# Sharing the place comparisons of an attention value pass between VectorE and GpSimd

## The reference, cut to what matters

```
score = einsum('ehd,ehd->eh', K[src], Q[dst]) / sqrt(32) + edge_bias
m = segment_max(score, dst)
ex = exp(score - m[dst])
denom = segment_sum(ex, dst)
attn = ex / denom[dst]
out = segment_sum(attn[:, :, None] * V[src], dst)
```

## Time and profile before

| | |
|---|---|
| Median of three timed runs | 7159.44 us |
| The profiled execution | 7132.51 us |
| Its span | 7130.8 us |
| GpSimd busy | 4465.6 us (63%) |
| TensorE busy | 4317.0 us (61%) |
| VectorE busy | 3165.0 us (44%) |
| Mean granted TensorE clock | 0.781 |

### The profile page before, as it was taken

How to read it: one execution, slowest core, us unless ns; L and a number is a source line. 1 busy time by engine, 2 the same in 40 slices (tenths; PEclk the granted TensorE clock), 3 DMA queues, 4 the chain that set the end, 5 groups by cost and what they waited for, 6 DMA issues and landing times. The chain is left out here.

```text
span 7130.8 us, 75257 instructions
## 1 busy us (share of the span) xinstructions
PE 4317.0 (61%) x20054; PEld 2955.9 (41%) x20055; DVE 3165.0 (44%) x6539; ACT 1916.6 (27%) x4343; POOL 4465.6 (63%) x4304
## 2 busy tenths in 40 slices
PE   1000588888766666668896455455477767775555
PEld 1000365656534444445674333233344434443333
DVE  5040345544446888878644222222244433333443
ACT  2630355555424555446461000000000000000000
POOL 2677566666546888746313666666566646665666
PEclk6555788888778899989997676767688878887766
DMA  3112122222105666657103445454455544443333
GB/s 85 46 41 54 55 65 67 66 66 67 42 25 178 210 210 213 189 168 215 43 0 122 145 147 140 147 147 146 129 170 176 176 114 133 131 134 97 97 97 87
DMA packets 466880, 826.73 MB, mean 116 GB/s; under 512 B 146229, under 2 KB 316182, under 8 KB 460057
## 3 DMA queue, kind: packets, MB, share of 16 engines
q0 software_dynamic: 209808, 566.12, 27.9%
q1 hardware_dynamic: 256777, 256.98, 11.3%
HBM read 664.90 MB, written 157.90 MB: 115 GB/s over the span
## 5 line engine op out<-in xcount | busy, mean ns | idle before, releaser
L1349 POOL DMA_INDIRECT p_rows<-table,idx_s x1320 | 1292.0, 979 | 773.7 <-issue 372.2
L1394 PE MATMUL p_psA<-p_rows,p_hot 128*128 128x256 bf16 (+1 forms) x4840 | 895.0, 349 | 602.1 <-DMA p_rows<-table,idx_s 401.7
L1394 PEld LDWEIGHTS p_psA<-p_rows,p_hot 128*128 128x128 bf16 (+1 forms) x4840 | 622.1, 134 | 856.2 <-issue 714.3
L585 POOL DMA_INDIRECT p_space<-h_table,p_space x440 | 451.6, 1026 | 289.5 <-issue 126.9
L571 POOL DMA_INDIRECT rec_s<-p_rec_out,p_row_s x416 | 429.8, 1033 | 283.0 <-ACT p_rec_out L696 138.3
L1349 POOL DMA_INDIRECT p_rows<-rel_table,edge_d x440 | 433.8, 986 | 254.0 <-issue 126.2
L655 PE MATMUL p_psW<-p_wf,p_upto 128*128 128x256 f32 x1760 | 480.1, 434 | 183.9 <-DVE p_upto L815 163.3
L376 POOL DMA_INDIRECT rec_d<-edge_d,norm x416 | 426.4, 1025 | 238.2 <-issue 125.3
L1557 POOL DMA_INDIRECT p_rows<-rel_table,edge_d x440 | 437.8, 995 | 219.3 <-issue 129.9
L1423 ACT ACTIVATE sums<-p_psA,inv_degree 128x256 f32<-128x256 f32 x75 | 35.6, 474 | 1850.7 <-DMA p_locs<-loc_rows 963.0
L1777 POOL DMA_INDIRECT p_kg<-kv_table,edge_d x440 | 425.1, 966 | 165.2 <-issue 111.6
(11 more groups left out here) (354 smaller groups left out, 8749.8 us busy)
## 6 DMA issues: line engine op xcount, KB each, us to landing
v_sorted<-p_kg SPq DMA_DIRECT2D x110, 512.0 KB
p_val<-v_sorted SPq DMA_DIRECT2D x110, 512.0 KB
rel_table<-p_o SPq DMA_DIRECT2D x50, 1024.0 KB
p_rows<-table,idx_s POOLq DMA_INDIRECT x1320
p_space<-rec_s SPq DMA_DIRECT2D x110, 136.0 KB
p_locs<-loc_rows SPq DMA_DIRECT2D x110, 128.0 KB, 4.3
p_rows<-rel_table,edge_d POOLq DMA_INDIRECT x880
p_rec_out<-edge_attr SPq DMA_DIRECT2D x103, 128.0 KB
```

The source lines that it names most:

```text
L585: pool.indirect_dma_start(msg[q][:, u, :], None, table, bass.IndirectOffsetOnAxis(ap=rec_i[q][:, u, S_IDX:S_IDX + 1], axis=0))\
L1349: pool.indirect_dma_start(rows[q][:, u, :], None, table, bass.IndirectOffsetOnAxis(ap=idx(n * U + u), axis=0))\
L1394: step = pe.matmul(psA[:, bass.ds(at[u], D)], hot[q][:, u, :], rows[q][:, u, c * D:(c + 1) * D], start=False, stop=(c == terms - 1), skip_ ...
```

## The change

VectorE compares the places of the even groups only, still six groups ahead. GpSimd compares those of the odd groups, with the same operation on the same operands, five groups ahead of its own products. The semaphore `shown` becomes two, one per engine, and both TensorE and SyncE wait for the one that belongs to their group.

```diff
+        shown = [s.sem(n) for n in ("shown_by_dve", "shown_by_pool")]
+
+        def wait_shown(engine, n):
+
+            engine.wait_ge(shown[n % 2], n // 2 + 1)
+
+        def show(engine, n):
+
+            engine.wait_ge(shown_in[n % LR], n // LR * 16 + 16)
+            if n >= TR:
+                engine.wait_ge(spread, n - TR + 1)
+            engine.tensor_scalar(hotT[n % TR][:, :, :], rows[n % LR][:, :, :], g.lane[:, 0:1], None, ALU.is_equal)\
+                .then_inc(shown[n % 2], 1)
...
                     if n >= LR:
-                        sp.wait_ge(shown, n - LR + 1)
+                        wait_shown(sp, n - LR)
...
-                unrolled(groups, [(0, weigh)])
+                def show_odd(n):
+                    if n % 2:
+                        show(pool, n)
+
+                unrolled(groups, [(5, show_odd), (0, weigh)])
...
-                    pe.wait_ge(shown, n + 1)
+                    wait_shown(pe, n)
...
-                def show(n):
-                    dve.wait_ge(shown_in[n % LR], n // LR * 16 + 16)
-                    if n >= TR:
-                        dve.wait_ge(spread, n - TR + 1)
-                    dve.tensor_scalar(hotT[n % TR][:, :, :], rows[n % LR][:, :, :], g.lane[:, 0:1], None, ALU.is_equal)\
-                        .then_inc(shown, 1)
+                def show_even(n):
+                    if n % 2 == 0:
+                        show(dve, n)
...
-                unrolled(groups, [(6, show), (5, join), (0, add(0)), (5, lower), (0, add(1)), (0, add(2)), (0, add(3)), (0, pick)])
+                unrolled(groups, [(6, show_even), (5, join), (0, add(0)), (5, lower), (0, add(1)), (0, add(2)), (0, add(3)), (0, pick)])
```

More of the change, by code:

```diff
@@ L1969, in value_pass @@
         shown_in = [s.sem(f"shown_in{q}") for q in range(LR)]
-        measured, hotted, shown, spread, joined, lowered, picked, expd, weighed, summed, added, blanked = (
-            s.sem(n) for n in ("measured", "hotted", "shown", "spread", "joined", "lowered", "picked", "expd", "weighed",
+        measured, hotted, spread, joined, lowered, picked, expd, weighed, summed, added, blanked = (
+            s.sem(n) for n in ("measured", "hotted", "spread", "joined", "lowered", "picked", "expd", "weighed",
                                "summed", "added", "blanked"))
+        shown = [s.sem(n) for n in ("shown_by_dve", "shown_by_pool")]
[7 more added lines that the diff above has]
+                .then_inc(shown[n % 2], 1)
         cleared, dve_step, ahead_in = s.sem("cleared"), s.sem("dve_step"), s.sem("ahead_in")
```

## The result

The changed kernel takes 7163.64 us in the median of 20 runs, the kernel before 7139.42 us in 20 runs beside it. The ratio is 1.0033 with a 95% interval of 1.0024 to 1.0042: about 24 us slower. The time lies inside the full range that was given, 7112 to 7182 us, but on the wrong side of before; the forecast was 11 us faster. The interval is 0.2% wide, so the sign can be told, although the change is smaller than the 0.5% that I had put as what a measurement can tell.

What follows compares the result with a forecast made beforehand. VectorE's chain bounds the stage at 5.92 us per period; the new loop of 4.9 + 0.8 = 5.7 us saves 0.22 us times 50, 11 us: 7159.4 - 11 = 7148 us, own range 7132 to 7162, full range 7112 to 7182.

Steps and rivals of the forecast that it cites:

- The bound before: Value stage: VectorE's own chain of eight additions, two comparisons, a join and a lower sets the period of 5.92 us.
- the 0.46 us per period that leave VectorE: Odd comparisons leaving VectorE cut its period from 5.92 to 5.46 us; times 50 periods, 23 us at most.
- The price of GpSimd's comparison, s: Time of one odd-group comparison on GpSimd, taken as 0.8 us between 0.62 and 1.57.
- The break-even at s = 1.02: GpSimd comparison time from which the changed kernel would be slower than before, in the forecast's order.
- The loop: VectorE's even comparison, expand, GpSimd's comparison, two products, next even comparison: 4.9 + s, 5.7 us per period.
- case B: GpSimd's comparison is slow, s = 1.57: loop 6.47 us, 27 us slower, 7187 us; chance 0.2.
- The stage's start: GpSimd's first comparisons fall in its idle time before the first exponents; no cost, or s once without this cover.
- case C: GpSimd's comparison starts before VectorE's lower, which stands still for s: period 6.23 us, 15 us slower, 7175 us; chance 0.2.
- the full gain: Rival A: loop 5.52 us or less, VectorE's 5.46 us the bound; 20 to 23 us faster, 7137 us; chance 0.17.
- Late places: Transfers for odd groups landing late: 5 us if one in ten is late; rival D, 7159 us, chance 0.08.
- The offset of 27 us between profile and median: Median of three timed runs lay 27 us above the profiled execution; the same offset was taken for the forecast.

Runs made afterwards that it cites:

- pair experiment: Kernel before, all comparisons on VectorE, but the odd one (seven groups ahead) directly behind the even one; ratio 0.9991 (0.9980 to 1.0002), period 5.73 us.
- the kernel with the comparisons in the gaps: Kernel before, all comparisons on VectorE, each moved into a wait between two additions; ratio 1.0081 (1.0064 to 1.0098), period about 7.0 us.

## Why the prediction was wrong

- **The bound before, and the 0.46 us per period that leave VectorE: right.** The pair experiment, where GpSimd is busy for only 65% of the time, gave 5.73 us (5.46 + 0.27). The 5.47 us of the kernel with more buffers agree with my 5.46, but prove less, since GpSimd's own work comes to 5.47 us there.
- **The price of GpSimd's comparison, s: this term failed.** I took 0.8 us between the bounds 0.62 and 1.57; it is 1.563. The upper bound came from the row of the same operation in the same type, 225 ns for one element and 370 for 56, and was exact within 0.01 us. I argued it away with its short rows and leaned on the memset and the affine select, which are other operations. The break-even at s = 1.02 lay between.
- **The loop: right in kind, 0.15 us too long.** I gave 4.9 + s; four kernels show 4.75 + s. The GpSimd comparison started 1.00 us after the products' end, not 1.07, and two products take 3.75 us from the comparison's end, not 3.83. With s = 1.563 my own sum gives 6.46 us and 27 us slower, case B, which had a chance of 0.2. Measured were 6.31 and 24. That 27 is so close to 24 is partly luck: the periods give only 20, and some 3 us come from the start of the stage.
- **The stage's start: a term that I had put at nothing.** I took GpSimd's first comparisons to fall into idle time. Two periods at the start cost 3.4 us more than before instead.
- **The lower's race, case C: the price was wrong.** I took it that VectorE's lower or comparison stands still beside any GpSimd instruction until that is over. It does beside a product. GpSimd's comparison holds it up only in its first half microsecond, by 0.43 us at most in the kernel with five hotT buffers, and not by s. So C's price of s on top doesn't exist, and the full gain was also to be had with s = 1.56 once the loop was open, which I hadn't seen.
- **Late places: near nothing.** In the changed kernel the places cost GpSimd 5.8 us of waiting, 4.0 of them in the stage's second period and 1.8 in one later period, of 7.12 us. They decide only with five hotT buffers.
- **The offset of 27 us between profile and median: wrong as an offset.** The kernel before had three runs then; with 20 its median is 7139, 7 us above the profiled one. It was the spread of the runs. It also lifted the predicted time: 11 us less than 7139 would have been 7128, and not 7148.

## What to carry to other kernels

Work given to an idle engine is paid by where it stands in the loops between engines, not by the idle time that it fills: ask for each new wait which instruction of the same period releases it, and whether that one can itself wait for the new work. Here more buffers, two of hotT and four of the places, turned 0.3% slower into 0.4% faster without another instruction. For a price that the trace doesn't show, take the row of the same operation and type, even a tiny one, before rows of the right size of another operation; and before giving work away, look whether the owner only does it at a bad moment.

## What the runs showed of the hardware

GpSimd's TENSOR_SCALAR takes 2.5 ns per element, by instructions of 256 and 512 elements in bf16 and of 256 in fp32, with a constant or a per-partition operand, so it is slower per element than GpSimd's two-input product (1.55 ns). The Trainium skill (GPSIMD Engine Reference, Performance versus the Vector engine) gives 769 ns for 512 elements at the best loop rate; the trace has 1563, and the measurement decides.

VectorE's comparison is held up by GpSimd's only near its start. In the kernel with more buffers of both kinds, one that starts 0.11 us into GpSimd's takes 0.72 us and one that starts 0.34 us into it 0.49 us; both end 0.83 us after the start of GpSimd's. One that starts 0.51 us or later into it takes the short duration, 0.34 to 0.35 us, in this kernel and in the one with five hotT buffers. Here is one that starts 0.34 us into GpSimd's comparison, and one that starts 0.90 us into it:

```profile
3269.77 1.56 POOL L1984 TENSOR_SCALAR p_hotT<-p_locs,lane 128x512 bf16<-128x512 bf16 x1
3270.11 0.49 DVE L1984 TENSOR_SCALAR p_hotT<-p_locs,lane 128x512 bf16<-128x512 bf16 x1
```

```profile
3263.37 0.48 DVE L2122 TENSOR_TENSOR p_theirs<-p_theirs,type_hot 128x320 f32<-128x320 f32 x1
3263.39 1.90 POOL L1984 TENSOR_SCALAR p_hotT<-p_locs,lane 128x512 bf16<-128x512 bf16 x1
...
3264.29 0.34 DVE L1984 TENSOR_SCALAR p_hotT<-p_locs,lane 128x512 bf16<-128x512 bf16 x1
```

In the second case GpSimd's comparison became longer, 1.90 us in place of 1.56, and a pick of VectorE had started just ahead of it. Where VectorE's comparison starts just ahead instead, GpSimd's takes 1.68 us. With five hotT buffers alone, a lower that starts 0.9 us into it goes with 1.60 us.

Beside a product the same comparison takes up to 1.99 us. The Trainium skill (SBUF — State Buffer, SBUF: two separate sides) has one rule for both, that whoever starts first keeps the shared pair for the whole instruction. The trace agrees for a product that has started first; GpSimd's comparison doesn't keep VectorE waiting to its end. Whether that comes from its one input or from its operation wasn't tried and stays open.

Between two products that follow each other at once, a VectorE comparison that has waited for some time gets in: in the kernel before, it starts 0.68 us before the first product's end and ends 0.14 us after it. One that starts less than 0.05 us before the first product's end doesn't, and takes 2.07 us, as in the kernel with the comparisons in the gaps.
